# Plain GRU steps and the quantised FFN in one block, the FFN cut into pieces between the steps' matmuls; silu as one ScalarE instruction

## The reference

```python
def cell(h, x):                                   # _L0_cond_ref, scanned over T = 64
    gi = x @ W_ih + b_ih
    gh = h @ W_hh + b_hh
    r = sigmoid(i_r + h_r); z = sigmoid(i_z + h_z)
    n = tanh(i_n + r * h_n)
    h_new = (1.0 - z) * n + z * h
...
qx, sx, sc = _reorder_quantize_x(xf, up_reorder_index)     # row scale from the row's largest |value|, rounding to fp8
g = _qlinear(qx, sx, sc, w_gate, ...)
u = _qlinear(qx, sx, sc, w_up, ...)
t = jax.nn.silu(g) * u
qt, st, sct = _reorder_quantize_x(t, down_reorder_index)
y = _qlinear(qt, st, sct, w_down, down_reorder_index)
x = x + y
```

## Time and profile before

| | us |
|---|---|
| median of 3 runs | 5771.4 (5770.47 to 5777.26) |
| the profiled execution: its time | 5770.47 |
| its span, first to last instruction | 5768.7 |
| first state product of the plain steps | 4515.3 |
| mean granted TensorE clock over the span | 0.911 |

### The profile page before, as it was taken

The page is one execution under the profiler, slowest core; times in us unless marked ns, Lnnn a source line. Parts: engine busy times, 40 slices in busy tenths (PEclk is TensorE's granted clock), DMA queues, the critical chain, the costliest instruction groups (busy, mean ns, idle before and its releaser), DMA issues. The chain is left out here.

```text
span 5768.7 us, 209967 instructions
## 1 busy us (share of the span) xinstructions
PE 4710.5 (82%) x93050; PEld 3029.9 (53%) x93050; DVE 2886.1 (50%) x5677; ACT 1486.4 (26%) x2964; POOL 1736.7 (30%) x801
## 2 busy tenths in 40 slices
PE   2699999999999999999989994664441799986565
PEld 1466666666766666666667773554330344432222
DVE  7344434436753444544464446335558211128887
ACT  4122222222222223522262221000004211114443
POOL 0333243333323331233204330443221000007776
PEclk7799999999999999999999997887775899998877
DMA  4211111111111111311131110332222100000111
GB/s 146 85 46 48 49 41 47 46 41 46 50 48 36 49 48 43 100 47 49 44 104 41 50 48 18 90 90 56 56 68 108 41 23 22 22 18 24 28 28 34
DMA packets 220282, 299.75 MB, mean 52 GB/s; under 512 B 38750, under 2 KB 172423, under 8 KB 219337
## 3 DMA queue, kind: packets, MB, share of 16 engines
q1 hardware_dynamic: 214185, 272.70, 16.6%
q10 hardware_dynamic: 3584, 9.44, 0.5%
q0 software_dynamic: 1760, 5.77, 0.3%
HBM read 252.07 MB, written 28.33 MB: 49 GB/s over the span
## 5 line engine op out<-in xcount | busy, mean ns | idle before, releaser
L654 PE MATMUL psum<-whole_w,whole_hot 128*32 128x384 f16 x49152 | 3007.8, 327 | 34.1 <-issue 34.1
L661 PE MATMUL psum<-low_w,low_hot 128*32 128x384 f16 x24576 | 2090.7, 327 | 0.0
L654 PEld LDWEIGHTS psum<-whole_w,whole_hot 128*32 128x32 f16 x49152 | 1359.1, 97 | 683.2 <-issue 36.9
L563 POOL TENSOR_TENSOR whole_hot<-whole_a,whole_mask 48x2048 f16<-48x2048 f16 x192 | 692.7, 3608 | 2198.1 <-PE psum L654 1612.7
L614 ACT ACTIVATE whole_w<-run_high 32x384 f16<-32x384 f32 x1488 | 776.6, 522 | 2195.2 <-DVE run_high L811 2182.2
L811 DVE TENSOR_SCALAR run_high<-psum 128x384 int32<-128x384 int32 x372 | 207.4, 558 | 1602.4 <-PE psum L654 1415.2
L661 PEld LDWEIGHTS psum<-low_w,low_hot 128*32 128x32 f16 x24576 | 679.3, 97 | 322.6
L818 DVE TENSOR_SCALAR whole_w<-psum 32x384 f16<-32x384 f32 x1488 | 822.7, 553 | 27.8
L701 PE MATMUL psum<-low_w,low_hot 64*64 64x384 f16 x12288 | 505.2, 324 | 11.9 <-POOL low_hot L575 7.1
L701 PEld LDWEIGHTS psum<-low_w,low_hot 64*64 64x64 f16 x12288 | 422.5, 108 | 94.7 <-issue 13.6
L575 POOL TENSOR_TENSOR low_hot<-low_a,sum_mask 128x1024 f16<-128x1024 f16 x128 | 242.5, 1895 | 516.8 <-DVE low_a L797 448.8
(11 more groups left out here) (279 smaller groups left out, 3596.5 us busy)
## 6 DMA issues: line engine op xcount, KB each, us to landing
whole_w<-w_rows SPq DMA_DIRECT2D x768, 72.0 KB
low_w<-w_rows SPq DMA_DIRECT2D x384, 144.0 KB
low_w<-w_rows SPq DMA_DIRECT2D x384, 120.0 KB
low_w<-w_rows SPq DMA_DIRECT2D x384, 72.0 KB
low_w<-w_rows SPq DMA_DIRECT2D x384, 48.0 KB
w_rows<-w_split SPq DMA_DIRECT2D x64, 144.0 KB
w_rows<-w_split ACTq DMA_DIRECT2D x64, 144.0 KB
work<-in_x SPq DMA_DIRECT2D x64, 128.0 KB, 2.6
```

The lines of the kernel that those rows point to most:

```text
L563: nc.gpsimd.tensor_tensor(whole_hot[part, buf].rearrange("p s k c -> p (s k) c"), whole_a[part, bass.ds(c, 1), :].to_broadcast([WHOLE_KIND ...
L654: last = nc.tensor.matmul(run[m][u][j * Q:(j + 1) * Q, :], whole_hot[:, buf, sign, kk, j % 2 * Q:(j % 2 + 1) * Q], whole_w[:, buf, u * 2 + ...
L661: nc.tensor.matmul(run[m][u][j * Q:(j + 1) * Q, :], low_hot[:, buf, kk, j % 2 * Q:(j % 2 + 1) * Q], low_w[:, buf, cols(j // 2, u)], start= ...
```

## The change

The two blocks become one. All states, those of the exact steps too, go to a DRAM tensor `all_states` and come back as tiles of 128 rows (`h_tile`, two buffers, one DMA a tile). The FFN's buffers move from `work` to `store`, since `work` still holds the GRU weights. FFN tile t is cut into pieces which each engine takes up between the parts of pair t of the plain steps (`next(ffn)`). There are 28 pairs and 32 tiles: tiles 28 to 31 and the drain run after the last pair (`last_tiles`). PSUM has 8 banks: gates take two instead of four (one buffer, so `input_open` now waits for this step's own `rz` and `pre`), `ps_g` and `ps_u` one each instead of three each (so chunk c of `gate_up` waits for VectorE to have read chunk c-1). The FFN's silu is one ScalarE instruction, VectorE makes u_t from the u sums and `up_row`, and GpSimd does one product a chunk.

```diff
-            gates = [psum[:, 0:2, :], psum[:, 2:4, :]]
+            gates = psum[:, 0:2, :]
+            ps_g = psum[:, 4, :]
+            ps_u = psum[:, 5, :]
...
+                    def tile_work(t):
+                        if live(t):
+                            gate_up(t, 0)
+                        yield
+                        if live(t - 2):
+                            down(t - 2)
+                        yield
+                        if live(t):
+                            gate_up(t, 1)
+                        yield
+                        yield
+                        if live(t):
+                            gate_up(t, 2)
+                        yield
+                        if live(t + 1):
+                            turn_state(t + 1)
+                        yield
+                        if live(t - 1):
+                            turn_t_first(t - 1)
+                        yield
+                        if live(t - 1):
+                            turn_t_rest(t - 1)
+                        yield
...
+                            pe.wait_ge(hT_ok, i * BODY + s + 1)
+                            state_part()
+                            next(ffn)
+                            if s % 2 == 0 and not (last and s == BODY - 2):
...
+                                turn_x((pair + 1) % 2)
+                            if more:
...
+                                pe.wait_ge(rz_ok, i * BODY + s + 1)
+                                pe.wait_ge(pre_ok, i * BODY + s + 1)
+                                input_open()
+                                input_part(nxt, 0)
+                            next(ffn)
+                            if more:
+                                input_part(nxt, 1)
+                            next(ffn)
+                            if more:
+                                input_part(nxt, 2)
+                            next(ffn)
+                            if more:
+                                pe.wait_ge(h_ok, i * BODY + s + 1)
+                                turn_h(s % 2)
+                                input_part(nxt, 3)
...
-                        nc.scalar.activation(sig[:, o:o + w], g_act[:, o:o + w], ACT.Sigmoid).then_inc(sig_ok, 1)
+                        nc.scalar.activation(silu_t[:, o:o + w], g_act[:, o:o + w], ACT.Silu).then_inc(silu_ok, 1)
...
+                    def tile_work(t):
+                        if live(t):
+                            silu(t, 0)
+                        yield
+                        if live(t):
+                            silu(t, 1)
+                        yield
+                        if live(t):
+                            silu(t, 2)
+                        if live(t + 1):
+                            state_copy(t + 1)
+                        if live(t - 1):
+                            t_copy(t - 1)
+                        yield
+                        if live(t):
+                            t_value(t, val, sc)
+                            t_value(t, vb, scg)
+                        if live(t + 2):
+                            state_values(t + 2)
+                        yield
...
-                                nc.gpsimd.tensor_tensor(sig[:, s], sig[:, s], up_row[:, s], ALU.mult).then_inc(sigu_ok, 1)
...
-                                nc.gpsimd.tensor_tensor(t_t[:, s], gu_t[:, s], sig[:, s], ALU.mult).then_inc(t_ok, 1)
+                        nc.gpsimd.tensor_tensor(t_t[:, s], u_t[:, s], silu_t[:, s], ALU.mult).then_inc(t_ok, 1)
...
-                            nc.vector.scalar_tensor_tensor(gu_t[:, s], ps_u[c][:, 0:w], hmx_keep[:], g_act[:, s],
+                        nc.vector.scalar_tensor_tensor(u_t[:, s], ps_u[:, 0:w], hmx_keep[:], up_row[:, s],
```

More of the change, by code:

```diff
@@ L1726, in build, with all_rounds, last_tiles, parts @@
             FIRST_TURN = 8
[L1728 to L1729 removed]
+            ROUNDS = (T - EXACT) // BODY
+            PAIRS = BODY // 2
+            def all_rounds(eng, work):
+                work(0, False)
+                work(1, False)
+                with eng.Fori(2, ROUNDS - 1) as i:
+                    work(i, False)
+                work(ROUNDS - 1, True)
+            def last_tiles(work):
+                for t in range(ROUNDS * PAIRS, NT + 2):
+                    work(t)
             def live(t):
                 return not isinstance(t, int) or 0 <= t < NT
[L1735 to L1742 removed]
+            def parts(w, k, half):
+                rz_w = w[:, k, 0:2 * D].rearrange("p (g s c) -> p g s c", g=2, s=2)[:, :, half, :]
+                n_w = w[:, k, 2 * D + half * HALF:2 * D + (half + 1) * HALF]
+                return rz_w, n_w
+            def finish(work):
+                for _ in work:
+                    pass
             with nc.Block() as block:
@@ new lines, in _, with work @@
+                    for half in range(2):
+                        sp.dma_start(h[half * B:(half + 1) * B, 1, :], all_states[EXACT - 1, :, half * HALF:(half + 1) * HALF]).then_inc(h0_in, 16)
+                    load_pair(0, 0)
+                    load_tile(0, 0)
+                    load_pair(1, 1)
+                    load_tile(1, 1)
+                    load_residual(0)
+                    sp.wait_ge(hm_ok, 1)
+                    load_tile(2, 0)
+                    def work(i, last):
+                        for s in range(BODY):
+                            if s % 2 == 0 and not last:
+                                sp.wait_ge(x_used, i * PAIRS + s // 2 + 1)
+                                load_pair(i * PAIRS + s // 2 + 2, s // 2)
+                            sp.wait_ge(h_ok, i * BODY + s + 1)
+                            store_state(i, s)
+                            if s % 2 == 1:
+                                next_tile(i * PAIRS + s // 2, s // 2)
+                                put_out(i * PAIRS + (s // 2 - 2))
@@ new lines, in _, with work, work_after @@
+                    for t in range(2):
+                        pool.wait_ge(tile_in[t], 16)
+                        need(pool, hval_ok, 2 * t)
+                        nc.gpsimd.tensor_tensor(hm, h_tile[t], up_used, ALU.mult).then_inc(hm_ok, 1)
+                    def work(i, last):
+                        for pair in range(PAIRS):
+                            tile_work(i * PAIRS + pair, pair, 16 * (i + 2))
+                    all_rounds(pool, work)
+                    def work_after(t):
+                        tile_work(t, t % 2, 16 * (t // 2 + 2))
@@ L1796, in _ @@
+                    last_tiles(work_after)
                 @block.vector
```

654 lines of the change are left out of this document (305 added, 349 removed).

## The result

| | before | changed |
|---|---|---|
| median of 4 runs each, us | 5773.58 (5770.47 to 5777.26) | 5516.97 (5512.80 to 5518.78) |
| ratio, 95% interval | | 0.9554 [0.9538, 0.9571] |
| span of the profiled execution, us | 5768.7 | 5515.8 |
| mean granted TensorE clock | 0.911 | 0.924 |

The change makes the kernel 4.5% faster. The forecast was 5496 with a range of 5470 to 5565: sign and range held, and the time is 21 us longer than forecast.

A forecast was written before the change was run, and what follows sets the result against it. TensorE was to bound the pairs: start 4515.3, plus 28 pairs x 31.6 = 884.8, less 5.4, plus a tail of 99, gives span 5494; with 1.8 outside the span and 0.9 to the median, 5496 us, range 5470 to 5565.

The forecast's parts named there:

- first state product: Start of the plain steps: TensorE's first product was to come as before, at 4515.3.
- tail: Tiles 28 to 31 alone after the last pair, to the end: 99 us together, bounds 82 and 120.
- The bound: Pairs with a tile: TensorE sets the time at full clock; VectorE, GpSimd and ScalarE fit under its 31.3 us.
- The wait for `pre` at the single gate buffer: Even step's `input_open`, which now needs this step's `pre`: the wait was to be covered by 1.3 us.
- The size of the pair: TensorE's work in two plain steps with a tile: 23.25 + 8.0 = 31.3 us, 31.6 with handoffs.
- six handoffs: Passing between pieces on TensorE: 0.3 us a pair added, bounds 0 and 0.6.
- rival A: The forecast itself: pairs of 31.0 to 32.2, tail 85 to 115, 5475 to 5515 us; chance 0.58.
- C: VectorE late for the odd opening by up to 2.3 us a pair, GpSimd's work under `t_round`: 5560; chance 0.14.
- E: FFN pieces cost TensorE more than counted (gate/up at 6.23, a wait at every piece): 33.5 a pair, 5550; chance 0.09.
- B: ScalarE table switch between busy instructions costs twice its row, some 2.6 us: 1.1 a pair, 5527; chance 0.15.
- D: Slower than before: waits between pieces lower TensorE's clock over the pairs; 62.6 a pair and 6370 at half clock; chance 0.04.
- The silu edit: FFN's silu: nothing from the edit itself was to reach TensorE; GpSimd's three fewer products a tile lie off the path.

The follow-up runs named there:

- e5: Changed kernel with only TensorE's order altered, FFN pieces beside other 128-column work, ten changes of form a pair for sixteen: 5497.63 us, pair 31.62.
- e1: Changed kernel with Sigmoid in place of Silu, leaving out the factor g, so no table loads in the pairs: 5513.51 us, pair 32.39.
- e7: Changed kernel with two one-column activations behind the silu of chunk 2, bringing two more table loads a pair: 5587.13 us, pair 34.36.
- e3: Changed kernel with silu in its old form (sigmoid, two GpSimd products a chunk), so the interleaving alone: 5527.15 us, pair 32.64.
- e0_again: The changed kernel run once more, unaltered, beside the other experiments: 5512.70 us, ratio 0.9551 to the kernel before.
- e4: Changed kernel with three more long-satisfied semaphore waits a step on TensorE, ahead of input chunks 1, 2 and 3: 5513.61 us, pair 32.39.

## Why the prediction was right, and what it missed

| term | predicted | measured | |
|---|---|---|---|
| first state product | 4515.3 | 4520.16 | +4.9, spread |
| 28 pairs with a tile | 28 x 31.6 | 28 x 32.39 | +22.1 |
| two pairs without down | -5.4 | -5.8 | -0.4 |
| tail | 99 | 94.6 | -4.4 |
| span | 5493.7 | 5515.8 | +22.1 |

**The bound** was right. TensorE, which bound the plain steps, bounds the pairs: no gap, clock 1.00, every piece of the chain TensorE's. The wait for `pre` at the single gate buffer does not appear.

**The size of the pair was the step that failed**: "TensorE's work in a pair with a tile is then 23.25 + 8.0 = 31.3" and the "0.3 a pair for six handoffs (bounds 0 and 0.6)". The chain gives the FFN's pieces 1.41 + 2 x 1.83 + 2.48 + 0.33 + 0.55 + 0.27 = 8.70 and the GRU's work 32.39 - 8.70 = 23.7, so both sides grew, by 0.65 and 0.45. Ten changes of form more than before (16 for 6) at 0.11 in the mean make the 1.1 that stand over 31.3 (8.0 of which is an estimate, so the 0.11 is no sharper than that; e5's 0.13 and the single places, 0.10 to 0.15, are measured). I had priced six handoffs at 0.05, with 0.6 a pair as the upper bound, and should have counted every piece twice, once going in and once coming back. The measured 32.39 a pair and 5517 us lie just above rival A's own band (31.0 to 32.2, 5475 to 5515): the range held because it took in parts of C and E. In e5 the four changes more than before all stand at the start of an FFN piece, the GRU's own parts have as many as before, and the GRU's work is 31.62 - 8.38 = 23.24, the 23.25 of the earlier trace rows. The rows shown held no such change: the earlier trace rows has `turn_x`, the opening and a chunk, where the extra lies inside the 0.66 and 1.05, unmarked, and I took the slopes of the earlier trace rows, which lie inside one form. E had the place right (dearer pieces) and the cause wrong: no wait at a piece, gate/up at its full-clock price.

**B, table loads twice their row**: false. e1 takes four away and e7 adds two; each is 1.28 and nothing else. The predicted slacks were 0.5 for `state_copy` and 0.1 behind the even step's `rz`; the trace has 0.7 and 0.3.

**C, VectorE late**: false for the changed kernel and true one product further. Predicted slack 0.4, measured 0.50 to 0.60; predicted price of a product 0.95, measured 1.06 on the first rounding instruction and 0.95 on the next (e3). The 2.3 us were too high a price even there: the pair grew by 0.25.

**D, the clock**: false, 1.00 in the pairs, and still 1.00 in e7 with TensorE idle 5.6% of the time. (By the prediction's own terms its time at half clock is 6364, not 6370.) In the tail the clock fell to 0.78, which the 99 us had in it.

**Tail**: 5421.23 to 5481.21 is three tiles of 20.0, as predicted. The last part, 5515.8 - 5481.21 = 34.6, was set at 39 and is the 4.4 too many.

**The silu edit** was called off the path in the pairs, and is nearly that: 0.25 a pair, 6.2 in the tail, 14.5 in all (e3 against e0_again). The prediction did not price it apart.

## What to carry to other kernels

Two stages that are bound by different engines gain by running side by side when the busy times of each engine fit under the one that has no gap; the gain is read from the shares per stage, and then the order decides whether it arrives. When work is cut into pieces between another's matmuls, compare the tile forms: every change between 64-column and 128-column weights is paid on both sides, so put pieces beside work of their own form. Before adding work to an engine, find the slack of each instruction that stands behind it: 0.5 to 0.6 us of idle time ahead of `rhn` was the whole difference between free and paid.

## What the runs showed of the hardware

- A change between 128x64 and 128x128 weight tiles cost 0.10 to 0.15 us on a full TensorE at clock 1.00 (0.13 in the mean of six, e5), between fp32 and fp16 as within fp32; the weight load then starts with the first matmul instead of 0.10 or more ahead of it. Six more satisfied semaphore waits a pair cost nothing (e4).
- A ScalarE table load took 1283 ns in the mean of 86 in 700 us, with 0.02 around it (e7, in a full queue).
- One GpSimd product of 128x512 fp32 that meets a VectorE instruction of 1408 columns lengthens that one by 1.06 (0.53 to 1.59, one input) or 0.95 (1.62 to 2.57, two inputs), about what is left of the product's 1.27 when the VectorE instruction starts.
